# A two-layer transformer on one core: the two late weight loads issued by ScalarE, nine expert tiles to two batches instead of five to each, and new places for all stages

## The reference

```python
x = x + L0_attn(xn, ...) + L0_ffn(xn, ...)      # xn = layernorm(x)
xn = layernorm(x)
x = x + L1_attn(xn, ...) + L1_ffn(xn, ...)
```

## Time and profile before

| | us |
|---|---|
| median of 3 runs | 1347.24 (1346.67 to 1348.15) |
| the profiled execution | 1351.91 |
| its span in the profile | 1350.1 |

### The profile page before, as it was taken

One profiled execution on the slowest core, in us unless ns is written; L12 is line 12 of the kernel. 1 busy time (PEld: TensorE's weight loads), 2 busy tenths in 40 slices (PEclk: granted clock), 3 DMA queues, 4 the chain that ended last, 5 costly groups with the idle time before them and its releaser, 6 DMA issues.

```text
span 1350.1 us, 29053 instructions
## 1 busy us (share of the span) xinstructions
PE 1176.1 (87%) x9951; PEld 683.3 (51%) x9951; DVE 929.1 (69%) x2183; ACT 849.8 (63%) x1349; POOL 545.9 (40%) x888
## 2 busy tenths in 40 slices
PE   5667899999989989676889999999999999999997
PEld 3333454444444544322355665665566566556654
DVE  2354677777777666586677877777777778777772
ACT  4236677777777776224467666766766676676665
POOL 2023343344433433322234444444544444444445
PEclk8779999999999999757699999999999999999999
DMA  3741445444444445543432334144323423432411
GB/s 115 172 101 34 113 106 126 110 114 124 114 107 107 108 120 127 124 101 147 103 58 48 42 53 60 27 59 60 58 33 55 60 43 46 58 55 32 57 18 20
DMA packets 102896, 108.69 MB, mean 81 GB/s; under 512 B 13272, under 2 KB 78680, under 8 KB 102488
## 3 DMA queue, kind: packets, MB, share of 16 engines
q1 hardware_dynamic: 82032, 94.17, 30.6%
q0 software_dynamic: 20720, 12.67, 7.7%
HBM read 73.09 MB, written 33.10 MB: 79 GB/s over the span
## 4 chain that ended last, share of the span: by engine, by line
PE 67%; DVE 11%; ACT 10%; issue 8%; POOL 3%; DMA 1%; SPq 0%; ACTq 0%; POOLq 0%; DVEq 0%
PE PS L744 10%; PE PS L627 9%; PE PS L777 8%; PE PS L579 7%; PE PS L729 6%; ACT flow L932 5%; PE PS L711 5%; PE PS L788 3%; PE PS L605 3%; PE PS L558 3%; DVE nm L1176 3%; PE PS L571 2%; PE PS L695 1%; POOL flow L1331 1%; PE PS L643 1%
## 5 line engine op out<-in xcount | busy, mean ns | idle before, releaser
L932 ACT ACTIVATE flow<-PS 128x1024 f32<-128x1024 f32 x320 | 321.9, 1023 | 131.1 <-PE PS L729 128.2
L1331 POOL TENSOR_SCALAR_AFFINE_SELECT flow<-flow 128x256 f32<-128x256 f32 (+1 forms) x448 | 229.1, 556 | 314.7 <-ACT flow L932 311.6
L1176 DVE TENSOR_REDUCE nm<-PS 128x2 f32<-128x1024 f32 x128 | 155.3, 1224 | 39.1 <-PE PS L695 37.6
L744 PE MATMUL PS<-flow 128*32 128x512 f32 (+3 forms) x2048 | 173.8, 459 | 9.5 <-POOL flow L1331 5.4
L1178 DVE TENSOR_REDUCE nm<-PS 128x2 f32<-128x768 f32 x128 | 121.9, 953 | 61.0 <-PE PS L695 57.1
L1363 POOL DMA_INDIRECT out_y<-ysb,rowu x71 | 112.8, 1589 | 100.8 <-DMA out_y<-X 56.3
L729 PE MATMUL PS<-qk 34*128 34x512 f16 (+3 forms) x1024 | 125.5, 311 | 31.4 <-ACT flow L932 12.3
L579 PE MATMUL PS<-xnT,up 128*128 128x512 f32 x288 | 150.0, 627 | 2.7 <-ACT xnT L831 2.2
L711 PE MATMUL PS<-qk 34*128 34x512 f16 (+3 forms) x1024 | 128.0, 315 | 25.4 <-ACT flow L932 11.5
L777 PE MATMUL PS<-xsT,w1s 128*128 128x128 f32 x1136 | 142.1, 279 | 0.0
L777 PEld LDWEIGHTS PS<-xsT,w1s 128*128 128x128 f32 x1136 | 136.0, 195 | 1.5
(11 more groups left out here) (182 smaller groups left out, 2130.6 us busy)
## 6 DMA issues: line engine op xcount, KB each, us to landing
early<-gate_rows SPq DMA_DIRECT2D x36, 512.0 KB, 7.7
qk<-gate_rows SPq DMA_DIRECT2D x28, 512.0 KB, 8.3
qk<-relay_q SPq DMA_DIRECT2D x64, 128.0 KB
qk<-relay_k SPq DMA_DIRECT2D x64, 128.0 KB
xsb<-xs SPq DMA_DIRECT2D x71, 65.0 KB
values<-vtmp SPq DMA_DIRECT2D x16, 256.0 KB
out_y<-X SPq DMA_DIRECT2D x16, 256.0 KB
relay_k<-qkh SPq DMA_DIRECT2D x32, 128.0 KB, 8.9
```

The source lines that it names most:

```text
L744: ins = pe.matmul(m.PS[32 * j:32 * j + 32, m.PV, kt * P:], m.vst[b % 2][:, kt, 4 * g + j, :], m.pt[:, r, k * L + o:k * L + o + L - kt * P] ...
L932: act.activation(m.pt[:, n % RING, :], m.PS[:, i:i + 2, :].rearrange("p k c -> p (k c)"), ACT.Exp, scale=1.0 / SCALE).then_inc(s["exp"], 1)
L1176: dve.tensor_reduce(nm[:, :, n, 3], ps, AX_X, ALU.max, negate=True).then_inc(s["max"], 1)
L1331: ins = pool.affine_select(part, part, [[0, part.shape[1]], [1, P]], ALU.is_ge, nothing, base=0, channel_multiplier=-1)
```

## The change

Three edits. First, the stages w1 and w2 go from the function of SP to that of ACT, with their waits and destinations unchanged. Second, TPB becomes 9, TBS = 2 is new and TB0 becomes 1: nine tiles are placed over two batches by nine numbers, and `among` follows (rounded up). The first tile stands beside batch 1's scores 15 and 16 (before: 12 and 13), and the last seven tiles come behind the last score of batch 15. Third, every table of places has new numbers, so that the order of the list changes in all parts: in OPENING the stages of batches 0 and 1 interleave, in the attention all numbers are some ten units later against the first half (rope(15,1), the last matmul of the first half, now stands ahead of all maxima), and the order within a batch of both halves differs. The set of stages is the same. In the tables of CLOSING, left out below, the same numbers stand as in ATTENTION but for relay, vload, vst and add (115.94 and 117).

```diff
--- before.py
+++ after.py
@@ FIRST, SECOND
-    stats0=[-40.55],
-    norm0=[-31.55],
-    xnT0=[-14.1],
-    kvr=[-5.55, -3.85, -3.15, -3.1],
-    up=[-12.9, -12.25, -7.8, -0.5, -0.15, 1.2, 1.95, 3, 3.05],
-    q=[-7.1],
-    kv=[-1.6],
-    route0=[-2.95],
-    gate=[-1.95],
-    attn0=[1.2],
-    gT=[0.45],
-    at0T=[3.9])
+    stats0=[-37.1],
+    norm0=[-30.1],
+    xnT0=[-15],
+    kvr=[-5.5, -4.9, -4.75, -4.55],
+    up=[-12.1, -11.85, -9.45, -6.75, -0.85, -0.55, 0.75, 3.55, 4.35],
+    q=[-6.15],
+    kv=[-1.65],
+    route0=[-4.35],
+    gate=[-3.3],
+    attn0=[2],
+    gT=[0.25],
+    at0T=[4.55])
...
-    x1=[18.35],
+    x1=[17.55],
...
-    rope=[23.65, 37.25],
-    parts=[29.95, 41.65],
+    rope=[24.65, 36.05],
+    parts=[33.4, 40.95],
...
@@ OPENING, batch 0
-    xnT0=[-520.85],
-    kvr=[-516.45, -499.75, -479.6, -430.2],
-    up=[-517.4, -511.75, -505.55, -487.65, -486.25, -462.65, -462, -456.15, -447.85],
...
-    down=[-212.55, -211.15, -205.65, -204.6, -199.5, -196, -195, -192, -190.95],
...
-    x1=[-96.2],
...
-    sort=[-15.75, 5.1, 13.4, 14.15],
+    xnT0=[-2360],
+    kvr=[-2316.85, -2255.85, -2252.2, -2162.9],
+    up=[-2347.4, -2276.65, -2113, -1528.35, -1501.45, -1255.6, -1222.2, -880.85, -719.75],
...
+    down=[-534.95, -519.6, -465.45, -411, -406.7, -351.1, -321.05, -296.05, -285.35],
...
+    x1=[-268.3],
...
+    sort=[21.7, 38.75, 40.65, 41.1],
@@ OPENING, batch 1 (20 units are added to each)
-    stats0=[-116.7],
-    norm0=[-103.2],
-    xnT0=[-94.35],
-    kvr=[-71.5, -62.8, -62.3, -51.3],
-    up=[-81.1, -79.15, -70.25, -67.05, -64.25, -51.45, -37.85, -27.35, -8],
-    q=[-53.05],
...
-    down=[-6.8, -5.85, -5.8, -5.6, -4.1, -4.05, -3.65, -2.4, -2.15],
...
-    x1=[6.6],
+    stats0=[-1004.65],
+    norm0=[-959.1],
+    xnT0=[-452.2],
+    kvr=[-411.8, -340.2, -278.55, -261.45],
+    up=[-260.15, -227.1, -209.45, -155.95, -110.7, -57.85, -18.65, -10.1, -9.95],
+    q=[-303.6],
...
+    down=[-31.35, 2.7, 3.5, 5.65, 6.95, 10.8, 13.4, 16.45, 17.2],
...
+    x1=[17.5],
@@ ATTENTION
-    score=[60.75, 60.95, 63.7, 64.75, 65.6, 67.3, 68, 68.3, 69.3, 69.8, 69.8, 70.1, 71.6, 74.5, 75.2, 77.8, 78.35,
-           78.45, 79.4, 80.05],
-    max=[49.2, 50.05, 50.65, 53.3, 54, 55.85, 57.45, 59.65, 60.1, 60.3, 61, 64.2, 65.65, 65.75, 66.25, 66.65, 66.95,
-         67.6, 67.7, 68.75],
-    mrows=[59.5, 61.85, 67.2, 72.45],
-    mlow=[59.75, 62.6, 67.45, 73],
-    value=[64.25, 67, 68.8, 71.7, 76.95, 79, 80.05, 83.7],
-    sums=[74.25, 82.85],
-    heads=[78.15, 85.3],
-    mT=[85.75],
-    out=[90.6],
-    relay=[40.75],
-    vload=[34.6],
-    vst=[50.85],
-    add=[105.8])
+    score=[71.52, 72.92, 73.02, 73.57, 73.67, 74.52, 76.02, 77.07, 77.62, 78.12, 78.22, 82.52, 83.37, 84.67, 86.47,
+           86.52, 88.32, 89.62, 90.47, 90.87],
+    max=[58.52, 61.02, 63.47, 63.97, 65.17, 65.22, 66.72, 67.72, 68.02, 68.87, 70.57, 71.37, 72.57, 73.07, 73.57,
+         74.42, 75.12, 76.62, 76.82, 77.62],
+    mrows=[69.82, 70.82, 75.02, 79.62],
+    mlow=[69.97, 70.97, 76.02, 79.62],
+    value=[74.87, 76.47, 78.57, 83.72, 86.82, 89.72, 90.82, 92.97],
+    sums=[85.62, 93.02],
+    heads=[92.37, 93.27],
+    mT=[94.42],
+    out=[103.22],
+    relay=[52.13],
+    vload=[57.2],
+    vst=[66.7],
+    add=[115.49])
...
@@ the tiles and the single stages
-TPB, TB0 = 5, 2
+TPB, TBS, TB0 = 9, 2, 1
 TILES = placed(
-    tile=[54.45, 60.7, 66.35, 67.95, 69.75])
+    tile=[88.25, 97, 98.05, 104.8, 105.45, 108.25, 116.95, 118, 126.35])
 
 END = placed(
-    w1=[72.4],
-    w2=[91.8],
-    tables=[61.8, 64.5, 70.9, 71.75, 73.7, 80.95],
-    pads=[78],
-    load=[84.1, 89.2, 89.4, 89.5, 91.85, 92.65])
+    w1=[56.75],
+    w2=[78.04],
+    tables=[67.26, 68.86, 71.47, 73.52, 77.02, 78.35],
+    pads=[70.65],
+    load=[103.4, 103.87, 104.55, 104.82, 105.69, 106.78])
 
 
 def among(b):
 
-    return min(NTILE, TPB * b + 1)
+    return min(NTILE, -(-TPB * b // TBS))
 
 
 def tile(n):
-    return S2 * (TB0 + n // TPB) + TILES[n % TPB][0]
+    return S2 * (TB0 + TBS * (n // TPB)) + TILES[n % TPB][0]
...
@@ scalar_program (the same two functions leave sync_program)
+    def w1(_, i):
+        act.wait_ge(s["downs"], B)
+        act.wait_ge(s["gated"], (NC - 1) * B)
+        act.dma_start(m.w1, io["w1"]).then_inc(s["d_w1"], 16)
+
+    def w2(_, i):
+        act.wait_ge(s["qk_mm"], 4 * B)
+        act.wait_ge(s["v_mm"], B)
+        act.wait_ge(s["ranks_mm"], B)
+        act.wait_ge(s["slots"], B)
+        act.wait_ge(s["d_sorted"], 16 * NT * B)
+        act.dma_start(m.w2[:, :], io["w2"]).then_inc(s["d_w2"], 16)
```

More of the change, by code:

```diff
@@ new lines @@
+    stats0=[-37.1],
[10 more added lines that the diff above has]
+    at0T=[4.55])
+SECOND = placed(
+    down=[5.9, 8.25, 8.55, 12.3, 14.35, 15.2, 15.55, 16.45, 17.55],
+    gated=[6.6, 7.25, 7.95, 8.65, 10.25, 10.3, 10.45, 13.4],
+    x1=[17.55],
+    stats1=[18.45],
+    norm1=[22.6],
+    xnT1=[23.7],
+    rope=[24.65, 36.05],
+    parts=[33.4, 40.95],
+    v=[29.5],
+    logits=[24.65],
+    route1=[26.2],
+    expert=[27.75],
+    ranks=[29.8],
+    sort=[26.25, 27.25, 30, 36.3],
+    vout=[36.4],
+    begun=[16.6])
@@ new lines @@
+OPENING = [placed(
+    stats0=[-3349.45],
+    norm0=[-2507.4],
+    xnT0=[-2360],
+    kvr=[-2316.85, -2255.85, -2252.2, -2162.9],
+    up=[-2347.4, -2276.65, -2113, -1528.35, -1501.45, -1255.6, -1222.2, -880.85, -719.75],
+    q=[-1747.3],
+    kv=[-1482.2],
+    route0=[-1274.85],
+    gate=[-1143.3],
+    attn0=[-843.15],
+    gT=[-976.05],
+    at0T=[-715.65],
+    down=[-534.95, -519.6, -465.45, -411, -406.7, -351.1, -321.05, -296.05, -285.35],
+    gated=[-676.6, -667.3, -587.95, -575.65, -496.25, -470.2, -444.55, -377.05],
+    x1=[-268.3],
+    stats1=[-190.55],
+    norm1=[-137.65],
+    xnT1=[-137.6],
+    rope=[-129.9, -37.3],
+    parts=[-45.65, 4.9],
+    v=[-4.7],
+    logits=[-125.5],
+    route1=[-75.65],
+    expert=[4.85],
+    ranks=[7.8],
+    sort=[21.7, 38.75, 40.65, 41.1],
+    vout=[0.95],
+    begun=[-81.25]), placed(
+    stats0=[-1004.65],
[4 more added lines that the diff above has]
+    q=[-303.6],
+    kv=[-161.65],
+    route0=[-154.85],
+    gate=[-94.95],
+    attn0=[-79.2],
+    gT=[-67.05],
+    at0T=[-35.4],
+    down=[-31.35, 2.7, 3.5, 5.65, 6.95, 10.8, 13.4, 16.45, 17.2],
+    gated=[-14.95, -9.3, 0.95, 2.8, 6.45, 6.8, 7.55, 9.6],
+    x1=[17.5],
+    stats1=[21.7],
+    norm1=[22.1],
+    xnT1=[23.85],
+    rope=[25.05, 35.75],
+    parts=[31.85, 40.9],
+    v=[26.8],
+    logits=[25.65],
+    route1=[26.55],
+    expert=[27.4],
+    ranks=[29.4],
+    sort=[27.2, 28.7, 29.55, 38.1],
+    vout=[31.6],
+    begun=[21.8])]
@@ L263 @@
 START = placed(
[L264 to L268 removed]
+    fill=[-1199.95, -1059.5],
+    casts=[-166.65],
+    rest=[-217.1])
+TPB, TBS, TB0 = 9, 2, 1
 TILES = placed(
[L270 removed]
+    tile=[88.25, 97, 98.05, 104.8, 105.45, 108.25, 116.95, 118, 126.35])
 END = placed(
[L273 to L277 removed]
+    w1=[56.75],
[3 more added lines that the diff above has]
+    load=[103.4, 103.87, 104.55, 104.82, 105.69, 106.78])
@@ L797, in tensor_program, with scalar_program @@
             share[name](b, i)
-def scalar_program(nc, m, s, order, work):
+def scalar_program(nc, m, s, io, order, work):
     act = nc.scalar
@@ L972, in casts @@
         act.copy(m.wo1[:, :], m.o16[:, :]).then_inc(s["casts"], 1)
-    share = dict(casts=casts, norm0=norm0, norm1=norm1, xnT0=xnT0, kvr=kvr, up=up, q=q, kv=kv, route0=route0, gT=gT, at0T=at0T, down=down, xnT1=xnT1, parts=parts,
+    share = dict(casts=casts, w1=w1, w2=w2, norm0=norm0, norm1=norm1, xnT0=xnT0, kvr=kvr, up=up, q=q, kv=kv, route0=route0, gT=gT, at0T=at0T, down=down, xnT1=xnT1, parts=parts,
                  v=v, vst=vst, route1=route1, mrows=mrows, score=scores, sums=sums, mT=mT, staged=staged, turned=turned,
@@ L1514, in rest @@
         sp.dma_start(m.X[:, 2 * NT:, :], m.x_d[:, 2:].rearrange("p b t d -> p (b t) d")).then_inc(s["d_restx"], 16)
-    share = dict(rest=rest, begun=begun, mlow=mlow, vout=vout, vload=vload, gT=gT, parts=parts, relay=relayed, w1=w1, w2=w2, pads=pads, load=load)
+    share = dict(rest=rest, begun=begun, mlow=mlow, vout=vout, vload=vload, gT=gT, parts=parts, relay=relayed, pads=pads, load=load)
     def consts(first, last, done):
@@ L1549, in program @@
         vector_program(nc, m, s, order, work)
-        scalar_program(nc, m, s, order, work)
+        scalar_program(nc, m, s, io, order, work)
         tensor_program(nc, m, s, order, work)
```

129 lines of the change are left out of this document (30 added, 99 removed).

## The result

The changed kernel takes 1368.25 us (median of 4 runs, 1361.96 to 1373.62), the kernel before 1347.70 beside it: ratio 1.0135, interval [1.0108, 1.0162]. The forecast was 1340.2, range 1316 to 1362: wrong in sign, and 6 us above the range. The profiled execution took 1366.43 us, span 1364.6.

A forecast was written before the change was run, and what follows sets the result against it. PE was taken as the bound, judged by its gaps. From the profiled 1351.9 us, -28 + 0 + 9.5 + 4.5 + 7 = -7 gave 1344.9, less 4.7 to the median gave 1340.2; range 1316 to 1362.

The forecast's parts named there:

- The opening: Start to x1(2): interleaving batches 0 and 1 brings x1(2) from 157 to 125 us; -28 us, bounds -33 and -16.
- First half, steady: First half's steady batches: table loads and cover stay, small waits offset each other; 0 us, bounds ±4 over 12.9 batches.
- Loads on ScalarE: w1 and w2 loads moved from SyncE's queue: only issue time on an idling ScalarE; 0, at most +0.7 us.
- The seam: Between the halves: first score at 597, first tile at 688, less work done ahead; +9.5 us, bounds +3 and +16.
- Second half, steady: Attention with tiles: hand-walked order idles 3.25 us a batch against 2.96; +4.5 us over 14.2 batches, bounds -20 and +25.
- The end: After the last score: seven tiles follow, 43 us with 16.7 lost against 9.9 before; +7 us, bounds +3 and +10.
- From the profiled execution to the median: Last step of the sum: median of plain runs taken as 4.7 us below the profiled execution, 1344.9 to 1340.2.
- the alternation bites: Rival, second half's tile-free runs: maxima share one PSUM pair, 4.6 us idle a batch, +19, 1359 us; chance 0.20.

The follow-up runs named there:

- e1: The kernel before with only the new placements of the first half; second half, tiles and w1/w2 loads as before: 1328.75 us, ratio 0.9833.
- e5: The kernel of e1 with w1 and w2 loaded on ScalarE's queue too: 1328.06 us, ratio 0.9855.
- e7: The changed kernel with five tiles in every batch, at the places of its own five-tile batches, first tile loads moved to fit: 1351.22 us, ratio 1.0009.
- e14: The kernel of e1 with two more DVE reductions a batch, one ahead of the sixth maximum, one ahead of the sixteenth: 1375.32 us, ratio 1.0218.
- e8: The changed kernel with the four transposes of heads done three times over: 1363.00 us, ratio 1.0125.
- e9: The kernel of e1 with nine tiles to two batches and the transposes of heads done three times over: 1377.71 us, ratio 1.025.
- e3: The changed kernel with only its nine tile places changed, spread evenly instead of in clusters: 1559.89 us, ratio 1.155.
- e4: The kernel before with only its five tile places changed, put in a cluster: 1551.60 us, ratio 1.151.

## Why the prediction was wrong

*The opening*: right. x1(0), x1(1) and x1(2) came at 53.1, 100.1 and 130.9 us, where 53, 94 and 125 plus 4 for half clock were forecast. That is -26.0 against -28, and e1 shows that it reaches the end.

*First half, steady*: 0 was forecast, +3.3 came (period 31.3 instead of 31.0 us), inside the bounds of 4. e1 has it too (401.8 us from x1(2) to x1(15), against 397.9), so it belongs to the new places of the first half; which of them costs it stays open.

*Loads on ScalarE*: right, by e5.

*The seam*: right. The first score came 40.6 us after x1(15) (forecast 597 against x1(15) at 554.87, so 42.1) and the first expert matmul 130.0 us after it (forecast 688, so 133.1); +6.2 in all against +9.5.

*Second half, steady*: the step that failed. Its walk was right: undisturbed periods of 46.65 and 43.88 us, a mean of 45.37 over the 13, against 45.3, and the waits that it named (DVE's maximum, the row maxima that come 2.5 us ahead of their score) stand in the trace. PE's time as the price of a tile was right too: at full clock a period with one tile fewer is 2.8 us shorter, of the tile's 3.14. The walk counted idle time only by its sum, 3.1 to 3.35 us a batch against 2.96, and priced each us of it at one us. That the steady stage would keep its clock of 1.00 was not a step at all: it was taken over from the kernel before without being named. It did not keep it. Nearly the same sum of idle time, placed otherwise in the period, brought 11 stretches at half clock, and they cost 19 us on top. The Trainium skill (TensorE: Matmul & The Clock Gate, A second HAM failure mode: psum-queue depth-cycling) describes a kernel whose clock swings because PE idles briefly and often between groups of matmuls; this trace agrees, with 11 falls behind waits of 0.60 to 0.74 us.

*The end*: right in kind. The last score came 45.6 us before the end (forecast 43), with add(15) between the scatters of tiles 67 and 68; +8.5 against +7. GpSimd's scatters wait for the transfer of X once, 4.1 us, instead of 56.3 us in all, as forecast. Tiles that follow one another alone there start 3.74 us apart, and 0.70 of it is a wait until DVE has scaled the outputs of the tile before (ysb).

*From the profiled execution to the median*: the forecast took off 4.7 us, and 1.8 would have had to be added. The 4.7 came from a single profiled execution, and a difference of this size between executions is not a property of the kernel.

*The rivals*: "the alternation bites" gave 1359 and decides above a period of 45.8; the period was 46.8. But its mechanism, 4.6 us idle from a single pair of banks, isn't what happened: undisturbed periods have 3.1 to 3.55 us. Half clock was weighed for the seam and the opening only, where the rows of before showed it.

## What to carry to other kernels

When an order is rearranged around TensorE, list its waits one by one and where they stand, not their sum: short waits that come together can cost a second time through the clock, even where the share of busy time stays the same. The longest wait is no better a guide than the sum: in e7 most falls stand behind waits no longer than those of the kernel before. Read the granted clock period by period in the profile of the changed kernel, before explaining a loss by waits. And try the parts of a change apart: here the first half's placements alone give 0.983 (e1; 0.986 with the loads on ScalarE, e5), the fastest version run, better than both kernels, while the second half's cost more than the first had gained.

## What the runs showed of the hardware

- In the steady stage of the changed kernel PE's clock fell to half 11 times behind waits of 0.60 to 0.74 us, with PE busy 93% of the stage; waits of 0.9 and 1.2 us elsewhere had no fall behind them. Each stretch at half clock lasted 3.4 or 6.8 us. They cost 1.7 us each on average (19 us for 11), and 1.5 us each in e14, where they lasted 3.4.
- Adding 16 transposes a batch beside these waits (e8, 28.4 us busy in the stage) took 10 of 11 falls away and made the stage no longer. Where they stood 3 us or more from the wait (e9), there were 4 falls instead of 6.
- A tile's place within a batch decides by over 10%: e3 and e4 moved nothing but tiles and took some 200 us more than the kernel before. DVE's waits for a tile's tanh grew from 8.9 to 64.9 us (e3) and from 10.4 to 36.5 us (e4) in 400 us, with maxima behind them.
- What exactly lets one thin place cause a fall and the next one not (11 of 35) stays open.
